# Routed experts with the first product two tiles ahead, two chunks to a PSUM bank and three banks for the second product

## The chip, the core and the metric

The kernel runs on one core of a Trainium2 chip. The metric is the time on the device in microseconds (us), the median of the runs. TensorE (PE in the rows) multiplies, VectorE (DVE), ScalarE (ACT) and GpSimd (POOL) work on what it leaves, SyncE (SP) starts transfers. The engines run programs of their own and meet at semaphores.

## What is computed

A layer of gated cross attention and a mixture of experts, on 32 sequences of 128 tokens with 128 channels (4096 tokens):

```python
x = x + tanh(g_xattn) * attention(layernorm(x), ctx, ctx, mask)      # 16 heads of 8
x = x + tanh(g_ffn) * ffn(layernorm(x))

def ffn(x):                                     # 2 shared experts, 8 routed ones, hidden size 512
    shared = mean over s of gelu(x @ sW1[s] + sb1[s]) @ sW2[s] + sb2[s]
    gates = x @ rW + rb
    w = softmax of the two largest gates, zero elsewhere
    moe = sum over e of w[e] * (gelu(x @ W1[e] + b1[e]) @ W2[e] + b2[e])
    return shared + moe
```

Only the two experts that a token chose are computed for it.

## The kernel before

The program has four stages: attention (with the gates), the shared experts, the routed experts, and the sum that ends the kernel. Every product of the experts is made of three matmuls in 16 bits: each operand is split into a high and a low half, and high times high, low times high and high times low are added in PSUM.

For the routed experts the rows of the tokens are scattered to slots in HBM, sorted by expert, each expert's slots filled up to a multiple of 256. That makes NTILE = 39 tiles of 256 slots, each of one expert, whose number stands in a register. For tile i:

- SP loads its rows into XR[i % 8] as soon as the results of tile i - 8 have been scattered (line 489).
- TensorE turns them into columns, four transposes into one PSUM buffer, rowT (`row_transposes`, line 1101). ScalarE copies them to XE[i % 3] (`routed_copy`, line 797). There is one rowT: the transposes of a tile wait until the tile before has been copied (semaphore XE).
- `routed_up`, line 1111, the first product: four chunks c of 128 hidden channels, three matmuls of 256 columns each. Chunk c goes to a PSUM bank of its own, pU[c] (pS0, pS1, pE0, pE1), in its first half. It waits for the activation of the same chunk of the tile before (semaphore gelu) and announces each chunk (semaphore up).
- `routed_gelu`, line 803: ScalarE takes each chunk to G32[i % 2], four activations of 128x256.
- `routed_split`, lines 1519 and 1521: VectorE makes high and low halves of two chunks at a time, in HR[i % 3] (semaphores hi, lo).
- `routed_down`, line 1123, the second product: 24 matmuls of 128 columns in pA[i % 2], the first 12 after the first half of the split, the rest after the second (semaphore dn).
- `routed_result`, line 1529: VectorE takes them to Y[i % 8] (semaphore y), and GpSimd scatters them with two indirect transfers (line 622) to HBM.

The order on each engine is written out by hand. I call it a step i. In step i TensorE does the first product of tile i + 1, the transposes of tile i + 3 and the second product of tile i; ScalarE the activations of tile i + 1 and the copy of tile i + 3; VectorE the split of tile i + 1 and the result of tile i.

Of the kernel before, what the change touches and what calls it, by code (L numbers as in the profile page):

```python
# [231 lines left out]
def layer(nc, io, k):  # L232
# [52 lines left out]
    G32 = [lt(f"G32{u}", [P, NC, TILE]) for u in range(2)]  # L285
    HR = [lt(f"HR{u}", [P, 2, NC, TILE], F16) for u in range(M)]
    Y = [lt(f"Y{u}", [P, 2, D]) for u in range(N)]
# [12 lines left out]
    pU = [wide(t) for t in (*pS, *pE)]  # L300
    pQK = lambda op: pM[:, 2 * op:2 * op + 2, :].rearrange("p a b -> p (a b)")
# [92 lines left out]
    with nc.Block() as block:  # L394
# [232 lines left out]
        def _(act):  # L627
# [166 lines left out]
            def routed_copy(i):  # L794
                act.wait_ge(r.T, i + 1)
                wait(act, r.up, NC * (i - M + 1))
                act.activation(XE[i % M][:], rowT, ACT.Copy).then_inc(r.XE, 1)

            def routed_gelu(i, e, c):
                act.wait_ge(r.up, NC * i + c + 1)  # L800
                if c % 2 == 0:
                    wait(act, r.lo, NC // 2 * (i - 2) + c // 2 + 1)
                act.activation(G32[i % 2][:, c, :], pU[c][:, 0:TILE], ACT.Gelu, bias=k.b1T[:, bass.ds(e * NC + c, 1)], scale=k.inv[:, 3:4]).then_inc(r.gelu, 1)  # L803

# [3 lines left out]
            for c in range(NC):  # L808
                routed_gelu(0, es[0], c)
            for i in range(NTILE):  # L810
# [16 lines left out]
        def _(pe):  # L827
# [276 lines left out]
            def routed_up(i, e):  # L1104
# [3 lines left out]
                for c in range(NC):  # L1108
                    wait(pe, r.gelu, NC * (i - 1) + c + 1)
                    for step, (w, part) in enumerate(((k.W1h, 0), (k.W1l, 0), (k.W1h, 1))):  # L1110
                        ins = pe.matmul(pU[c][:, 0:TILE], w[:, bass.ds(e * HID + c * P, P)], XE[i % M][:, part, :], start=(step == 0), stop=(step == 2))  # L1111
                    ins.then_inc(r.up, 1)

            def routed_down(i, e):
                wait(pe, r.y, i - 1)
                if i == 0:
                    pe.wait_ge(h.ot, NGR)
                for c in range(NC):
                    if c % 2 == 0:
                        pe.wait_ge(r.lo, NC // 2 * i + c // 2 + 1)  # L1120
                    for q in range(2):
                        for step, (w, part) in enumerate(((k.W2h, 0), (k.W2l, 0), (k.W2h, 1))):
                            ins = pe.matmul(pA[i % 2][:, q, :], HR[i % M][:, part, c, q * P:(q + 1) * P], w[:, bass.ds(e * HID + c * P, P)],  # L1123
# [9 lines left out]
            routed_up(0, es[0])  # L1133
            for i in range(NTILE):
# [7 lines left out]
        def _(v):  # L1142
# [371 lines left out]
            def routed_split(i):  # L1514
                for half in range(2):
                    ch = slice(2 * half, 2 * half + 2)
                    v.wait_ge(r.gelu, NC * i + 2 * half + 2)
# [107 lines left out]
```

## Time and profile before

| what | us |
|---|---|
| median of 3 runs | 527.5 (526.09 to 529.23) |
| profiled execution, its span | 524.9 |
| attention, ahead of the shared experts | to about 260 |
| shared experts | to about 362 |
| routed experts, the 39 tiles | 364.7 to about 504 |
| last scatters, loads and sums | to 524.9 |

A page of a profile gives the share of the span in which each engine is busy. Beside it stand views of the same execution by stretch, by wait, and in order of time. A wait is put down to whoever ended it; "issue" is an engine that waited for nothing the profile shows, and "remote" or "another core or an unknown queue" is a release for which the profile has no record at that time. The start of a matmul is recorded, its end is modelled. 2.6 us lie between the span and the median.

### The profile page before, as it was taken

What the parts mean: (1) busy time and instruction counts of PE and PEld (TensorE: products, weight loads), DVE (VectorE), ACT (ScalarE), POOL (GpSimd) and SP (SyncE); (2) the same over time, 40 slices, a digit from 0 to 9 for tenths busy, and PEclk for the clock granted to TensorE, in tenths of its full rate; (3) what the DMA queues carried; (4) which work ended last, traced back from release to release, by engine and by line L of the source; (5) the groups of instructions that cost most, each with busy time, mean ns of one, the idle gap of its engine ahead of it and who ended that gap; (6) DMA issues with size and microseconds to landing.
All of it is one profiled execution on the core that took longest, in us unless ns stands there. A gap on an engine that the chain in (4) does not pass through costs nothing.

```text
span 524.9 us, 13531 instructions
## 1 busy us (share of the span) xinstructions
PE 415.9 (79%) x4611; PEld 297.2 (57%) x4611; DVE 397.8 (76%) x983; ACT 340.8 (65%) x674; POOL 315.9 (60%) x382
## 2 busy tenths in 40 slices
PE   0377979879998989776784989898999989998930
PEld 0245767758776877554341433344878777776720
DVE  7696769868778778987774896494888768886795
ACT  0536857657787877665663876495677567765743
POOL 9151524494987889598876376650466656666550
PEclk9998989899999999988997989999999999999985
DMA  8767863442333534540011011113122222244119
GB/s 226 223 197 202 223 146 80 103 101 75 78 87 84 114 82 142 178 164 17 26 51 45 27 41 41 47 36 81 36 78 77 70 72 86 67 132 138 58 44 280
DMA packets 71753, 53.19 MB, mean 101 GB/s; under 512 B 7473, under 2 KB 63548, under 8 KB 71688
## 3 DMA queue, kind: packets, MB, share of 16 engines
q1 hardware_dynamic: 64608, 42.96, 30.2%
q0 software_dynamic: 4544, 8.44, 4.6%
q10 hardware_dynamic: 2536, 0.94, 0.7%
q8 instruction: 39, 0.64, 0.6%
q14 instruction: 26, 0.21, 0.2%
HBM read 29.38 MB, written 24.33 MB: 102 GB/s over the span
## 4 chain that ended last, share of the span: by engine, by line
PE 25%; DVE 8%; issue 5%; another core or an unknown queue 5%; ACT 4%; POOL 2%; DMA 1%; ACTq 0%; DVEq 0%; POOLq 0%
PE pAtt L1123 9%; PE pE L1111 4%; PE pS L1111 4%; DVE HH L1490 3%; PE pAtt L1061 2%; PE pMix L1101 2%; PE pS L999 2%; ACT H L767 1%; POOL yd L622 1%; PE pE L999 1%; DVE HH L1486 1%; ACT G L803 1%; DMA YY<-yd 1%; DVE t_X L1543 1%
## 5 line engine op out<-in xcount | busy, mean ns | idle before, releaser
L622 POOL DMA_INDIRECT yd<-Y,XR x78 | 85.0, 1089 | 72.5 <-DVE Y L1529 45.4
L1234 DVE TENSOR_REDUCE t_MX<-pS 128x4 f32<-128x512 f32 x128 | 86.4, 682 | 24.0 <-PE pS L861 22.4
L720 ACT ACTIVATE PT<-pE,t_mbias,t_scl 128x512 f32<-128x512 f32 x128 | 97.1, 788 | 6.6 <-PE pE L861 6.4
L597 POOL DMA_INDIRECT xs<-t_STG,t_pos x64 | 64.2, 1002 | 36.5 <-issue 15.4
L1123 PE MATMUL pAtt<-t_W2h,HR 128*128 x624 | 65.3, 219 | 6.8 <-issue 5.5
L803 ACT ACTIVATE G<-pS,t_b1T,t_inv 128x256 f32<-128x256 f32 x78 | 40.0, 569 | 43.6 <-remote 39.3
L1490 DVE SCALAR_TENSOR_TENSOR HH<-H,t_sc,HH 128x512 f16<-128x512 f32 x64 | 48.4, 761 | 21.6 <-ACT HH L772 14.7
L1521 DVE SCALAR_TENSOR_TENSOR HR<-G,t_sc,HR 128x512 f16<-128x512 f32 x78 | 58.6, 751 | 2.8
L1123 PE MATMUL pAtt<-t_W2l,HR 128*128 x312 | 56.4, 219 | 3.4 <-issue 3.4
L1123 PEld LDWEIGHTS pAtt<-t_W2h,HR 128*128 128x128 f16 x624 | 50.0, 97 | 12.6 <-issue 10.9
L861 PE MATMUL pE<-t_Q,t_K 128*128 128x128 f16 x512 | 51.6, 225 | 5.8 <-DMA t_Q<-MPT 4.8
L861 PE MATMUL pS<-t_K,t_Q 128*128 128x128 f16 x512 | 51.2, 225 | 4.1 <-DVE t_MX L1234 3.9
L1519 DVE TENSOR_SCALAR HR<-G,t_sc 128x512 f16<-128x512 f32 x78 | 37.5, 480 | 11.1 <-ACT G L803 11.1
L861 PEld LDWEIGHTS pE<-t_Q,t_K 128*128 128x128 f16 x512 | 37.1, 101 | 12.2 <-DMA t_Q<-MPT 5.3
L1061 PE MATMUL pAtt<-HH,t_W2h 128*128 128x512 f16 x128 | 38.2, 380 | 5.9 <-DVE HH L1490 3.6
L898 PE MATMUL pAtt<-PT,t_V 128*32 128x128 f32 x1024 | 42.8, 287 | 0.0
L522 POOL CAST QKS<-QK 128x512 f16<-128x512 f32 x16 | 9.8, 610 | 53.8 <-ACT QK L638 53.8
L803 ACT ACTIVATE G<-pE,t_b1T,t_inv 128x256 f32<-128x256 f32 x78 | 40.2, 578 | 0.0
L861 PEld LDWEIGHTS pS<-t_K,t_Q 128*128 128x128 f16 x512 | 34.6, 101 | 8.7 <-DVE t_MX L1234 7.8
L767 ACT ACTIVATE H<-pS,t_b1T,t_inv 128x512 f32<-128x512 f32 x32 | 23.6, 777 | 20.0 <-remote 13.6
L1529 DVE SCALAR_TENSOR_TENSOR Y<-pAtt,t_down,t_b 128x256 f32<-128x256 f32 x39 | 18.7, 480 | 20.5 <-remote 19.5
L1111 PE MATMUL pE<-XE,t_W1h 128*128 128x256 f16 x156 | 33.8, 274 | 0.0
(276 smaller groups left out, 1044.5 us busy)
## 6 DMA issues: line engine op xcount, KB each, us to landing
xs<-t_padrow SPq DMA_DIRECT2D x10, 516.0 KB, 5.3
XR<-xs SPq DMA_DIRECT2D x39, 129.0 KB
scr<-QKS SPq DMA_DIRECT2D x16, 256.0 KB, 2.2
t_Q<-scr SPq DMA_DIRECT2D x16, 256.0 KB
t_K<-scr SPq DMA_DIRECT2D x32, 128.0 KB
t_STG<-in_W SPq DMA_DIRECT2D x7, 512.0 KB, 6.4
YY<-yd SPq DMA_DIRECT2D x14, 256.0 KB, 5.8
t_X<-in_x SPq DMA_DIRECT2D x4, 512.0 KB, 6.5
```

Of the source, the lines that this page charges most:

```text
L597: g.indirect_dma_start(k.xs, bass.IndirectOffsetOnAxis(ap=pos[:, n:n + 1], axis=0), k.PAY[:, n, :], None).then_inc(h.di[q], 16)
L622: g.indirect_dma_start(k.yd, bass.IndirectOffsetOnAxis(ap=XR[u][:, q, D:ROW], axis=0), Y[u][:, q, :], None, bounds_check=2 * T - 1, oob_is ...
L720: act.activation(PT[:, m % NPT], pE[g % 2][:], ACT.Exp, bias=k.mbias[:, bt:bt + 1], scale=k.scl[:, bt:bt + 1]).then_inc(s.exp, 1)
L803: act.activation(G32[i % 2][:, c, :], pU[c][:, 0:TILE], ACT.Gelu, bias=k.b1T[:, bass.ds(e * NC + c, 1)], scale=k.inv[:, 3:4]).then_inc(r.g ...
L861: ins = pe.matmul(out[:, j, :], ko if transposed else qo, qo if transposed else ko, start=True, stop=True)
L898: ins = pe.matmul(pA[bb][32 * j:32 * j + 32, part // 2, :], k.V[pair % NB][:, 4 * bb + j, part, :], PT[:, m % NPT, j, :], start=(part == 0 ...
L1061: ins = pe.matmul(wide(pA[u]), w[:, w0:w0 + P], HH[e][:, part, c, :], start=(e == 0 and c == 0 and step == 0), stop=(e == 1 and c == NC - ...
L1111: ins = pe.matmul(pU[c][:, 0:TILE], w[:, bass.ds(e * HID + c * P, P)], XE[i % M][:, part, :], start=(step == 0), stop=(step == 2))
L1123: ins = pe.matmul(pA[i % 2][:, q, :], HR[i % M][:, part, c, q * P:(q + 1) * P], w[:, bass.ds(e * HID + c * P, P)], start=(c == 0 and q == ...
L1234: v.tensor_reduce(out=MX[:, n % G // 4, m % 2, m // 2::2], in_=pS[n % 2][:], axis=AX_X, op=ALU.max).then_inc(s.max, 1)
L1490: v.scalar_tensor_tensor(out=HH[e][:, 1, c, :], in0=H32[:, c, :], scalar=k.sc[:, 2:3], in1=HH[e][:, 0, c, :], op0=ALU.mult, op1=ALU.subtra ...
L1521: v.scalar_tensor_tensor(out=HR[i % M][:, 1, ch, :], in0=G32[i % 2][:, ch, :], scalar=k.sc[:, 2:3], in1=HR[i % M][:, 0, ch, :], op0=ALU.mu ...
```

## The change

Three things are done together, all in the routed stage:

- TensorE and ScalarE work two tiles ahead of the second product. In step i TensorE does the first product of tile i + 2, the transposes of tile i + 4 and the second product of tile i; ScalarE the activations of tile i + 2 and the copy of tile i + 4; VectorE the split of tile i + 2 and the result of tile i.
- The first product puts two chunks into one bank: a tile fills two of the four banks, and even and odd tiles use different pairs. It announces two chunks at a time and waits for two at a time, of tile i - 2. ScalarE waits and announces likewise, still with four activations.
- The second product goes round three banks (pA0, pA1, pO), G32 gets a third buffer and HR a fourth. They lie in tiles of the shared experts (pO, H32, HH0), so each waits once, at its first use, until that stage is done with it.

XR and Y stay at eight buffers, XE at three, rowT at one. The count of matmuls, activations and vector instructions is the same.

```diff
+    G32.append(H32[:, :, 0:TILE])
+    HR.append(HH[0][:, :, :, 0:TILE])
+    NG, NH = len(G32), len(HR)
...
+    up_out = lambda i, c: pU[i % 2 * 2 + c // 2][:, c % 2 * TILE:(c % 2 + 1) * TILE]
+    down_out = lambda i: (*pA, pO)[i % 3][:, 0:2, :]
...
             def routed_gelu(i, e, c):
-                act.wait_ge(r.up, NC * i + c + 1)
+                if i == 2 and c == 0:
+                    act.wait_ge(h.lo, NC * SUNITS)
                 if c % 2 == 0:
-                    wait(act, r.lo, NC // 2 * (i - 2) + c // 2 + 1)
+                    act.wait_ge(r.up, NC // 2 * i + c // 2 + 1)
+                    wait(act, r.lo, NC // 2 * (i - NG) + c // 2 + 1)
...
             for i in range(NTILE):
-                if i + 1 < NTILE:
+                if i + 2 < NTILE:
                     for c in range(NC):
-                        routed_gelu(i + 1, es[i + 1], c)
-                if i + 3 < NTILE:
-                    routed_copy(i + 3)
+                        routed_gelu(i + 2, es[i + 2], c)
+                if i + 4 < NTILE:
+                    routed_copy(i + 4)
...
                 for c in range(NC):
-                    wait(pe, r.gelu, NC * (i - 1) + c + 1)
+                    if c % 2 == 0:
+                        wait(pe, r.gelu, NC // 2 * (i - 2) + c // 2 + 1)
...
-                        ins = pe.matmul(pU[c][:, 0:TILE], w[:, bass.ds(e * HID + c * P, P)], XE[i % M][:, part, :], start=(step == 0), stop=(step == 2))
-                    ins.then_inc(r.up, 1)
+                        ins = pe.matmul(up_out(i, c), w[:, bass.ds(e * HID + c * P, P)], XE[i % M][:, part, :], start=(step == 0), stop=(step == 2))
+                    if c % 2:
+                        ins.then_inc(r.up, 1)
...
             def routed_down(i, e):
-                wait(pe, r.y, i - 1)
+                wait(pe, r.y, i - 2)
+                if i == 2:
+                    pe.wait_ge(h.x, NGR)
...
             for i in range(NTILE):
-                if i + 1 < NTILE:
-                    routed_up(i + 1, es[i + 1])
-                if i + 3 < NTILE:
-                    row_transposes(i + 3)
+                if i + 2 < NTILE:
+                    routed_up(i + 2, es[i + 2])
+                if i + 4 < NTILE:
+                    row_transposes(i + 4)
                 routed_down(i, es[i])
...
+            routed_split(1)
             for i in range(NTILE):
-                if i + 1 < NTILE:
-                    routed_split(i + 1)
+                if i + 2 < NTILE:
+                    routed_split(i + 2)
                 routed_result(i, es[i])
```

TensorE at the head of step 33, before (the last matmul of the second product of tile 32, then the first product of tile 34; XE and pS, pE are numbered by buffer):

```order
L1123 MATMUL pAtt0<-t_W2h,HR2 128x128
L1111 ISA [waits x_gelu,x_XE]
L1111 MATMUL pS0<-XE1,t_W1h 128x256
L1111 REGISTER_ALU
L1111 MATMUL pS0<-XE1,t_W1l 128x256
L1111 MATMUL pS0<-XE1,t_W1h 128x256
L1111 ISA [waits x_gelu]
L1111 MATMUL pS1<-XE1,t_W1h 128x256
```

The same place after, where the first product is that of tile 35:

```order
L1139 MATMUL pOut<-t_W2h,HR0 128x128
L1124 ISA [waits x_gelu,x_XE]
L1124 MATMUL pE0<-XE2,t_W1h 128x256
L1124 REGISTER_ALU
L1124 MATMUL pE0<-XE2,t_W1l 128x256
L1124 MATMUL pE0<-XE2,t_W1h 128x256
L1124 ISA
L1124 MATMUL pE0<-XE2,t_W1h 128x256
```

Chunks 0 and 1 share pE0, and the wait for an activation stands before every second chunk.

TensorE in the middle of step 33, before: the end of the first product of tile 34, the transposes of tile 36 (rows of XR4), the start of the second product of tile 33:

```order
L1111 MATMUL pE1<-XE1,t_W1h 128x256
L1101 MATMUL pMix<-t_ident16,XR4 128x128 [waits x_XE,x_ld4]
L1101 MATMUL pMix<-t_ident16,XR4 128x128 x3
L1123 REGISTER_ALU [waits x_lo,x_y]
L1123 MATMUL pAtt1<-t_W2h,HR0 128x128
```

The same place after: first product of tile 35, transposes of tile 37 (XR5), second product of tile 33:

```order
L1124 MATMUL pE1<-XE2,t_W1h 128x256
L1113 MATMUL pMix<-t_ident16,XR5 128x128 [waits x_XE,x_ld5]
L1113 MATMUL pMix<-t_ident16,XR5 128x128 x3
L1139 REGISTER_ALU [waits x_lo,x_y]
L1139 MATMUL pAtt0<-t_W2h,HR1 128x128
```

The transposes have moved with the first product, by one tile, and still wait for the copy of the tile before theirs.

ScalarE around the activations of tile 16, before; the last row is the copy of tile 18:

```order
L797 ACTIVATE XE2<-pMix 128x512 [waits x_up,x_T]
L803 ISA [waits x_lo,x_up]
L803 ACTIVATE G320<-pS0,t_b1T,t_inv 128x256
L803 ISA [waits x_up]
L803 ACTIVATE G320<-pS1,t_b1T,t_inv 128x256
L803 ISA [waits x_lo,x_up]
L803 ACTIVATE G320<-pE0,t_b1T,t_inv 128x256
L803 ISA [waits x_up]
L803 ACTIVATE G320<-pE1,t_b1T,t_inv 128x256
L797 ACTIVATE XE0<-pMix 128x512 [waits x_up,x_T]
```

And after:

```order
L802 ACTIVATE XE2<-pMix 128x512 [waits x_up,x_T]
L810 ISA [waits x_lo,x_up]
L810 ACTIVATE G321<-pS0,t_b1T,t_inv 128x256
L810 ISA
L810 ACTIVATE G321<-pS0,t_b1T,t_inv 128x256
L810 ISA [waits x_lo,x_up]
L810 ACTIVATE G321<-pS1,t_b1T,t_inv 128x256
L810 ISA
L810 ACTIVATE G321<-pS1,t_b1T,t_inv 128x256
L802 ACTIVATE XE0<-pMix 128x512 [waits x_up,x_T]
```

In both the copy of tile 18 stands behind the activations of tile 16: both moved by one tile against the second product, neither against the other.

## Rows read from the trace of the kernel before

**Rows 1.** The page: span, and TensorE's busy time, share and instructions

```profile
span 524.9 us, 13531 instructions
...
PE 415.9 (79%) x4611; PEld 297.2 (57%) x4611; DVE 397.8 (76%) x983; ACT 340.8 (65%) x674; POOL 315.9 (60%) x382
```

**Rows 2.** Stretch of three tiles: length, engines' busy time, granted clock, DMA, GB/s

```profile
398.00:408.67 10.67, 9.85 (x124) 8.21 (x122) 8.25 (x16) 7.14 (x15) 6.55 (x7) 1.00 0.25 76
```

**Rows 3.** Chain of waits, 421 to 440 us: start, length, what (instructions)

```profile
425.94 0.66 PE pS L1111 x6
...
427.48 1.34 PE pAtt L1123 x24
428.82 0.66 PE pS L1111 x6
...
430.35 0.40 PE pAtt L1123 x7
430.75 0.41 issue
...
431.56 0.32 issue
...
432.76 0.14 issue
432.90 0.85 PE pS L1111 x6
...
434.66 0.38 PE pMix L1101 x4
435.03 1.58 PE pAtt L1123 x24
436.62 0.65 PE pS L1111 x6
```

**Rows 4.** Who waited for whom, 366 to 502: us, times, longest

```profile
ACT G L803 <- remote: 39.3, 12, 3.6
DVE Y L1529 <- remote: 19.5, 12, 1.7
```

**Rows 5.** ScalarE in order of time: start, length, instruction, [idle before]

```profile
428.22 0.61 ACT L797 ACTIVATE XE<-pMix 128x512 f16<-128x512 f16 x1
432.09 1.02 ACT L803 ACTIVATE G<-pS,t_b1T,t_inv 128x256 f32<-128x256 f32 x2 [3.27 <-remote]
...
433.90 0.61 ACT L797 ACTIVATE XE<-pMix 128x512 f16<-128x512 f16 x1
```

**Rows 6.** VectorE in order of time, the same three tiles

```profile
429.69 0.75 DVE L1521 SCALAR_TENSOR_TENSOR HR<-G,t_sc,HR 128x512 f16<-128x512 f32 x1
432.05 0.48 DVE L1529 SCALAR_TENSOR_TENSOR Y<-pAtt,t_down,t_b 128x256 f32<-128x256 f32 x1 [1.60 <-remote]
```

**Rows 7.** GpSimd in order of time, first scatters of two tiles in a row

```profile
426.10 1.26 POOL L622 DMA_INDIRECT yd<-Y,XR  x1 [1.00 <-issue]
...
428.95 1.17 POOL L622 DMA_INDIRECT yd<-Y,XR  x1 [0.30 <-issue]
```

**Rows 8.** Shared experts in order of time: TensorE's last matmul, ScalarE's next activation

```profile
337.25 0.38 PE L1061 MATMUL pAtt<-HH,t_W2l 128*128 128x512 f16 x1
...
338.37 0.78 ACT L767 ACTIVATE H<-pS,t_b1T,t_inv 128x512 f32<-128x512 f32 x1 [6.38 <-remote]
```

**Rows 9.** Load of tile 8's rows as issued, and its transposes, in order of time

```profile
376.53 0.36 SPq L489 DMA_DIRECT2D XR<-xs  x1
...
384.30 0.39 PE L1101 MATMUL pMix<-t_ident,XR 128*128 128x128 f16 x4
```

**Rows 10.** The page's DMA issues: count, KB each, median us from issue to landing

```profile
YY<-yd SPq DMA_DIRECT2D x14, 256.0 KB, 5.8
...
scr<-QKS SPq DMA_DIRECT2D x16, 128.0 KB, 2.3
```

More of the change, by code:

```diff
@@ L809, in _ @@
                 routed_gelu(0, es[0], c)
+            routed_copy(3)
+            for c in range(NC):
+                routed_gelu(1, es[1], c)
             for i in range(NTILE):
-                if i + 1 < NTILE:
+                if i + 2 < NTILE:
                     for c in range(NC):
-                        routed_gelu(i + 1, es[i + 1], c)
-                if i + 3 < NTILE:
-                    routed_copy(i + 3)
+                        routed_gelu(i + 2, es[i + 2], c)
+                if i + 4 < NTILE:
+                    routed_copy(i + 4)
             for n in range(NQ):
@@ L1122, in routed_down @@
                         for step, (w, part) in enumerate(((k.W2h, 0), (k.W2l, 0), (k.W2h, 1))):
-                            ins = pe.matmul(pA[i % 2][:, q, :], HR[i % M][:, part, c, q * P:(q + 1) * P], w[:, bass.ds(e * HID + c * P, P)],
+                            ins = pe.matmul(down_out(i)[:, q, :], HR[i % NH][:, part, c, q * P:(q + 1) * P], w[:, bass.ds(e * HID + c * P, P)],
                                             start=(c == 0 and q == 0 and step == 0), stop=(c == NC - 1 and step == 2), skip_group_check=True)
@@ L1516, in routed_split @@
                     ch = slice(2 * half, 2 * half + 2)
-                    v.wait_ge(r.gelu, NC * i + 2 * half + 2)
-                    wait(v, r.dn, i - M + 1)
-                    v.tensor_scalar(HR[i % M][:, 0, ch, :], G32[i % 2][:, ch, :], k.sc[:, 2:3], None, ALU.mult).then_inc(r.hi, 1)
+                    v.wait_ge(r.gelu, NC // 2 * i + half + 1)
+                    wait(v, r.dn, i - NH + 1)
+                    if i == NH - 1:
+                        v.wait_ge(h.dn, SUNITS)
+                    v.tensor_scalar(HR[i % NH][:, 0, ch, :], G32[i % NG][:, ch, :], k.sc[:, 2:3], None, ALU.mult).then_inc(r.hi, 1)
                     v.wait_ge(r.hi, 2 * i + half + 1)
-                    v.scalar_tensor_tensor(out=HR[i % M][:, 1, ch, :], in0=G32[i % 2][:, ch, :], scalar=k.sc[:, 2:3], in1=HR[i % M][:, 0, ch, :],
+                    v.scalar_tensor_tensor(out=HR[i % NH][:, 1, ch, :], in0=G32[i % NG][:, ch, :], scalar=k.sc[:, 2:3], in1=HR[i % NH][:, 0, ch, :],
                                            op0=ALU.mult, op1=ALU.subtract).then_inc(r.lo, 1)
@@ L1528, in routed_result @@
                 row = k.b2[:, bass.ds(e * D, D)].rearrange("p (o d) -> p o d", o=1)
-                v.scalar_tensor_tensor(out=Y[u][:], in0=pA[i % 2][:, 0:2, :], scalar=k.down[:, 0:1], in1=row.to_broadcast([P, 2, D]),
+                v.scalar_tensor_tensor(out=Y[u][:], in0=down_out(i), scalar=k.down[:, 0:1], in1=row.to_broadcast([P, 2, D]),
                                        op0=ALU.mult, op1=ALU.add).then_inc(r.y, 1)
```

8 lines of the change are left out of this document (6 added, 2 removed).

## The prediction

> **What bounds the kernel now.** I began with the page: TensorE is busy 79% of the span, more than any other engine [rows 1], and the change touches nothing ahead of the routed stage. So I read that stage alone, first cut into stretches. Stretches of 10.67 us look alike from 377 to 494 us, and each holds three tiles, at a granted clock of 1.00, that is 2.4 GHz [rows 2]. In one of them the engines work 9.85 us (TensorE), 8.25 (VectorE), 7.14 (ScalarE) and 6.55 (GpSimd): none is full, TensorE nearly.
>
> The chain of waits shows what one such stretch is made of [rows 3]. First products begin at 425.94, 428.82, 432.90 and 436.62, so the three intervals are 2.88, 4.08 and 3.72 us. The first is TensorE back to back: 1.31 for the first product, 0.22 for the transposes, 1.34 for the second product. If every interval were 2.88, the stretch would take 8.64; it takes 10.68. **2.04 us are lost every three tiles**, and only that can be won.
>
> Where do they go? The views of waits name it: ScalarE waits 12 times, 39.3 us in all, on "remote", and VectorE waits 12 times, 19.5 us, on the same [rows 4]. In the stretch shown the first product of a tile starts at 428.82 and its first chunk is through by about 429.2. ScalarE has been free since its copy of 428.22, yet starts on that chunk at 432.09, after 3.27 us of idleness [rows 5]. VectorE finishes its split at 430.44 and starts the result of the tile before at 432.05, though that tile's second product was recorded as over at 428.82 [rows 6]. Both wait for semaphores that TensorE sets, and both get them at the same moment. So once in three tiles what TensorE has finished is announced some 3 us late. I call this the **late release**. TensorE itself goes on for a while in its records, then stops twice inside the second product, 0.41 and 0.32 us, for nothing the profile shows, and then goes at ScalarE's pace: 0.14 us of waiting, 1.76 instead of 1.31 for the next first product, 0.38 instead of 0.22 for the transposes, 1.59 instead of 1.34 for the second product behind them [rows 3].
>
> The Trainium skill says in Perfetto Trace Analysis, Tensor Engine Instruction, that the recorded end of a matmul is an estimate and that the semaphore goes out only when PSUM has acknowledged the writes. The rows agree that recorded end and release are two things; that they can lie 3 us apart no page told me.
>
> **The change, part by part.** The number of matmuls, activations, splits and scatters is the same, so the busy times stay. What it takes away or adds:
>
> *Waits of the first product.* Now each chunk waits for the same chunk of the tile before; after the change, for a pair of chunks two tiles back. In the stretch this removes the 0.14 and the 0.45 (1.76 less 1.31) that follow the late release [rows 3].
>
> *The transposes.* This is the wait that takes its place. Transposes of tile i + 4 need the copy of tile i + 3, which ScalarE makes behind the activations of tile i + 1. Before, those of tile i + 3 needed the copy of tile i + 2, behind the activations of tile i. In both, TensorE may be ahead of ScalarE by one tile less a first product, and no more. With the release at 432.09 as now, the four activations and the copy end at 433.90 + 0.61 = 434.51 [rows 5]. The transposes then start at about 434.60, where today they start at 434.66. Two tiles of lead, and the transposes move by 0.06 us.
>
> *The second product.* It is no longer paced by a split that has only just come: 1.34 instead of 1.59. The transposes take 0.22 instead of 0.38. So the next first product but one starts at 434.60 + 0.22 + 1.34 = 436.16 instead of 436.62 [rows 3]: **0.46 us gained per late release**. The two stops inside the second product, 0.73 us, don't count, either way: they lie before 434.60, where ScalarE is later than TensorE.
>
> *VectorE and GpSimd.* VectorE needs 8.25 us for three tiles [rows 2], 2.75 a tile. GpSimd begins two tiles in a row at 426.10 and 428.95 [rows 7], 2.85 a tile. Both are below 2.88, so neither sets a pace slower than TensorE's. But they are so near that a faster stage than 2.88 isn't to be had, and after a late release VectorE catches up only slowly. That costs nothing while its split is a tile ahead of the second product, which the fourth HR gives.
>
> *Two chunks at once.* ScalarE may start 0.33 us later on a tile, half of a pair's 0.66 [rows 3]. It has 7.14 of work in 10.67 us and a lead of a tile, so this is hidden, except behind a late release, where both chunks are long through. I take zero; the bound is 12 times 0.33, 4 us.
>
> *The ends.* At the start one more first product, 1.31 us, stands before the first second product. At the end two second products run with nothing between. The amount of work is the same, so I take zero, bounds -1 and +1.3. The one-time waits for pO, H32 and HH0 are on work of the shared stage that is over before tile 2 gets there: zero.
>
> *The loads of the rows.* The transposes come one tile earlier against the second product, while the load still waits for the scatter of eight tiles before. For tile 8 the load is issued at 376.53 and used at 384.30 [rows 9], 7.8 us later. One tile of 3.56 less leaves 4.2. No row gives the landing of these 129 KB; 128 KB of another kind take 2.3 and 256 KB 5.8 [rows 10]. By size it is nearest to the first: it fits. The second would not.
>
> **The sum.** 12 late releases times 0.46 are 5.5 us. On the profiled execution 524.9 - 5.5 = 519.4; the median of the runs lies 2.6 above its span, so 527.5 - 5.5 = **522.0**.
>
> **The rivals.**
>
> *The late release is absorbed.* If it has to do with how ScalarE and TensorE meet chunk by chunk, or ends earlier when TensorE waits less, all intervals become 2.88: 12 times 2.04 are 24.5 us, **503.0**. For it: two of three tiles already run near that pace, and half of the announcements and waits go. Against it: rowT keeps the two engines coupled, and the late release isn't seen to follow from a wait.
>
> *It isn't late at all: TensorE's work truly takes 10.67 us for three tiles*, and its records run ahead of it. Then nothing that reorders its work helps, **527.5**. For it: semaphores are what the other engines see. Against it: the release is prompt for two tiles in three, and between the releases there is not time enough for more. The Trainium skill gives a price by which this would be so, in TensorE: Matmul & The Clock Gate, Back-to-back issue gap: about 81 ns for a matmul of 128 columns with its weights. The 24 of the second product would take 1.9 us by it; the row says 1.34 for the 24 [rows 3].
>
> *The late release grows with TensorE's lead.* In the shared stage ScalarE waited 6.38 us for one and got it at 338.37, 0.74 us after TensorE's last matmul ended (337.25 + 0.38) and it had nothing more to do [rows 8]. If the release comes only when TensorE stops, a longer lead makes it later. TensorE would now run on to the transposes, at 428.82 + 2.88 + 1.31 = 433.01; the release would come at 433.75, activations and copy would end 2.42 later at 436.2, and 3.2 us would be lost instead of 2.04: 12 times 1.16 more, 13.9, **541.4**. It decides as soon as the release follows TensorE's stop. Against it: in the stretch shown TensorE stops in the middle of a product, where nothing asks it to.
>
> *The loads come too late.* If the rows land later than 4.2 us after issue, TensorE waits for them at the transposes. Four steps lie between a result and the transposes that reuse its place, so a lateness of x costs x/4 a tile. Landing at 5.0 us gives 0.2 a tile, over 37 tiles 7.4 less the 5.5 gained: **529.4**; at 5.8 it is 0.4 a tile, 14.8 less 5.5, 536.8.
>
> **How the numbers follow.** The forecast of 522.0 gets 0.40, with a range of its own from 518 to 526 (the zero terms above are its bounds). Absorbed: 0.20. TensorE truly full: 0.17. Grows with the lead: 0.13. Loads late: 0.10. 0.5% is 2.6 us, about what a measurement of this kernel can tell from no change. Faster by more: 0.37 of the forecast and the 0.20, 0.57. Within: 0.03 of the forecast and the 0.17, 0.20. Slower: 0.23. The range from 502 to 534 takes in the absorbed case and the late loads but for their worst, and leaves out 0.13 and a little.
>
> **What would show it.** In the profile after, the stretches should still repeat every three tiles, in about 10.2 us. ScalarE should still wait 12 times about 3 us for a release without a record. TensorE should no longer wait before the first product but before the transposes, for the copy, once in three tiles. The second product should take 1.34 everywhere. If ScalarE's unexplained waits are gone, the first rival holds; if stretches take 10.67 with TensorE waiting for nothing, the second; if the waits are longer than 4 us, the third; if the transposes wait for a transfer, the fourth. The forecast is wrong above all if the release isn't tied to a time but to what TensorE does next.

## The result

The changed kernel takes 531.25 us (median of 19 runs, 526.21 to 536.13) against 528.33 us before (19 runs, 525.99 to 535.18). The ratio is 1.0046, with a 95% interval of 1.0024 to 1.0068: by it 2.4 us slower, where 5.5 us faster had been forecast.

The page of the changed kernel, its first line and its line of busy times, answers to [rows 1]:

```profile
span 534.4 us, 13529 instructions
...
PE 414.2 (78%) x4611; PEld 301.9 (56%) x4611; DVE 398.4 (75%) x983; ACT 341.5 (64%) x674; POOL 315.5 (59%) x382
```

This execution was a disturbed one (granted clock 0.937, against 0.955 in the profile of before), so its span isn't compared, and only what repeats inside the stage is read from it. Who waited for whom, 370 to 511 us (total, times, longest), answers to [rows 4]:

```profile
ACT H L810 <- remote: 37.1, 11, 4.5
...
DVE Y L1549 <- remote: 17.1, 11, 1.8
```

The late releases are still there, eleven instead of twelve and about as long. The chain of waits of one stretch of three tiles (start, length, what) answers to [rows 3]:

```profile
443.48 0.51 issue
443.99 0.38 PE pMix L1113 x4
444.38 1.39 PE pAtt L1139 x24
445.77 1.31 PE pS L1124 x12
447.08 0.22 PE pMix L1113 x4
447.30 1.34 PE pOut L1139 x24
448.64 1.31 PE pE L1124 x12
...
454.26 0.54 issue
454.79 0.38 PE pMix L1113 x4
```

First products take 1.31 us each and no longer wait; TensorE now waits in front of the transposes, 0.51 and 0.54 us. So far it is what the forecast described, but for the transposes and the second product behind the wait, which take 0.38 and 1.39 us and not 0.22 and 1.34. But from transposes to the same transposes it is 454.79 - 443.99 = 10.80 us, not 10.2. The line that explains it wasn't TensorE's. GpSimd in order of time, the same stretch, answers to [rows 7]:

```profile
446.11 1.26 POOL L627 DMA_INDIRECT yd<-Y,XR  x1 [1.00 <-issue]
447.68 0.98 POOL L627 DMA_INDIRECT yd<-Y,XR  x1 [0.30 <-issue]
448.96 1.17 POOL L627 DMA_INDIRECT yd<-Y,XR  x1 [0.30 <-issue]
450.44 0.98 POOL L627 DMA_INDIRECT yd<-Y,XR  x1 [0.30 <-issue]
453.42 1.21 POOL L627 DMA_INDIRECT yd<-Y,XR  x1 [2.00 <-DVE Y L1549]
```

And ScalarE's first activations behind two late releases in a row:

```profile
441.43 1.93 ACT L810 ACTIVATE H<-pS,t_b1T,t_inv 128x256 f32<-128x256 f32 x4 [3.23 <-remote]
...
452.23 1.93 ACT L810 ACTIVATE H<-pE,t_b1T,t_inv 128x256 f32<-128x256 f32 x4 [3.26 <-remote]
```

Four scatters run back to back, from 446.11 to 451.42; the release comes at 452.23, 0.81 us after the last of them has ended. Then GpSimd waits for a result, which VectorE couldn't make before the release. Of this **train of four** the forecast had seen only that 2.85 us a tile is less than 2.88.

### The profile page after: what moved, and what is told of

It is laid out like the page before. It is cut to its first block, busy times and chain, and to the rows that moved or that the text cites. A ratio compares the mean times of both kernels' runs of the same rounds, so it can differ in the third digit from the quotient of the medians.

```text
span 534.4 us, 13529 instructions
## 1 busy us (share of the span) xinstructions
PE 414.2 (78%) x4611; PEld 301.9 (56%) x4611; DVE 398.4 (75%) x983; ACT 341.5 (64%) x674; POOL 315.5 (59%) x382
## 4 chain that ended last, share of the span: by engine, by line
PE 32%; DVE 22%; ACT 11%; issue 10%; another core or an unknown queue 8%; DMA 7%; POOL 4%; SPq 1%; ACTq 1%; DVEq 0%; POOLq 0%
PE pAtt L1139 4%; DVE HH L1508 4%; PE pS L1124 3%; DVE t_MX L1252 3%; DMA kwm<-t_tops 3%; PE pE L1124 3%; PE pAtt L910 3%; ACT G L810 2%; PE pE L873 2%; ACT H L772 2%; PE pS L873 2%; PE pMix L854 2%; PE pOut L1139 2%; PE pAtt L1073 1%
## 5 line engine op out<-in xcount | busy, mean ns | idle before, releaser
L910 PE MATMUL pAtt<-PT,t_V 128*32 128x128 f32 x1024 | 43.9, 292 | 0.0
L1139 PE MATMUL pAtt<-t_W2h,HR 128*128 x320 | 33.6, 220 | 4.1 <-issue 4.0
L1124 PE MATMUL pS<-XE,t_W1h 128*128 128x256 f16 x160 | 31.9, 285 | 0.6 <-issue 0.6
L1011 PE MATMUL pS<-t_STG,t_W1h 128*128 128x512 f16 x64 | 23.8, 411 | 10.1 <-ACT H L772 10.1
L1139 PE MATMUL pAtt<-t_W2l,HR 128*128 x160 | 29.2, 220 | 2.9 <-issue 2.9
L1541 DVE SCALAR_TENSOR_TENSOR HR<-G,t_sc,HR 128x512 f16<-128x512 f32 x40 | 30.0, 751 | 1.4
L1139 PEld LDWEIGHTS pAtt<-t_W2h,HR 128*128 128x128 f16 x320 | 25.7, 98 | 7.5 <-issue 7.4
L910 PEld LDWEIGHTS pAtt<-PT,t_V 128*32 128x32 f32 x1024 | 25.4, 114 | 7.2 <-issue 1.0
L810 ACT ACTIVATE G<-pE,t_b1T,t_inv 128x256 f32<-128x256 f32 x52 | 25.5, 580 | 4.7 <-PE pE L1124 2.6
L1124 PE MATMUL pE<-XE,t_W1h 128*128 128x256 f16 x152 | 28.0, 273 | 0.0
```

Source lines behind the costliest of these rows:

```text
L810: ins = act.activation(G32[i % NG][:, c, :], up_out(i, c), ACT.Gelu, bias=k.b1T[:, bass.ds(e * NC + c, 1)], scale=k.inv[:, 3:4])
L910: ins = pe.matmul(pA[bb][32 * j:32 * j + 32, part // 2, :], k.V[pair % NB][:, 4 * bb + j, part, :], PT[:, m % NPT, j, :], start=(part == 0 ...
L1124: ins = pe.matmul(up_out(i, c), w[:, bass.ds(e * HID + c * P, P)], XE[i % M][:, part, :], start=(step == 0), stop=(step == 2))
L1139: ins = pe.matmul(down_out(i)[:, q, :], HR[i % NH][:, part, c, q * P:(q + 1) * P], w[:, bass.ds(e * HID + c * P, P)], start=(c == 0 and q ...
```

## What the experiments had to tell apart

The experiments ran on seven chips, and these are of two kinds. On four (besides that of the first result) the kernel before takes 525.6 to 533.0 us, on three 484.1 to 486.4, and one of the three gave 484.14 and 485.13 at two times. Both kinds run the same program. I call them **chips of 526** and **chips of 486**. Every time below stands beside that of the kernel before on the same chip.

Theories: (a) TensorE's work truly takes 10.67 us for three tiles; (b) its sequencer is the limit, which computes an address for every matmul of the routed stage; (c) GpSimd's scatters hold up its semaphores; (d) it takes the other engines' work on PSUM; (e) the single buffer rowT holds back the lead, as the forecast said; and for the loss, (f) late loads and (g) the ends of the stage.

### TensorE alone

```diff
-                wait(pe, r.XE, i)
+                wait(pe, r.XE, min(i, 3))
-                    wait(pe, r.gelu, NC * (i - 1) + c + 1)
+                    if i == 1:
+                        pe.wait_ge(r.gelu, c + 1)
-                wait(pe, r.y, i - 1)
...
-    HR[i % M][:, part, c, q * P:(q + 1) * P]
+    HR[0][:, part, c, q * P:(q + 1) * P]
```

and the loops of the other engines over the tiles end after the first ones, so what such a kernel returns isn't the layer's result. Three such kernels ran on chips of 486:

> The kernel before, in whose routed stage only TensorE goes through all 39 tiles: transposes, first and second products as before, in the same order, but on the rows, the XE and the HR of the first tiles, so that after tile 0 it waits for nobody. Copies, activations and splits after the first tiles, results, scatters and all but the first eight loads are left out; the last stage adds up other data. Theory 'TensorE is full' (its work truly takes 10.67 us for three tiles): the 38 tiles behind the first take 3.56 us each also when nobody holds it up, first product to first product, some 135 us. Theory 'the late release comes from outside TensorE' (from another engine's or a queue's work, or from the way it meets ScalarE): 2.88 us each, some 109 us, in the records as in what the last semaphore tells, whose waiters are the loads of the last stage. Where the records run ahead of the truth, the loads begin later than the last recorded matmul by more than the 1 us that a semaphore and a DMA start may take.

> As the run with TensorE alone, but the weights of both products stand at a fixed place (expert 0) rather than at one computed from a register; the same parts are left out. If TensorE's sequencer is the limit (it computes an address for every matmul of the routed stage, 36 a tile), the tiles become shorter than in that run, by up to the 3.56 to 2.88 us. If it is the array or the loading of weights, both runs have the same length per tile.

> TensorE alone in the routed stage once more (the same parts left out as in the first run of it), wanted on a chip on which the kernel before takes some 526 us. Theory 'it is TensorE itself that stops on such a chip, whatever the others do': the 38 tiles take 3.56 us each, 135 us, seen at the latest in the time between the first routed product and the loads of the last stage, which wait for its last semaphore. Theory 'it takes the other engines': 2.87 us each, 109 us.

And one on a chip of 526:

> TensorE alone in the routed stage (the same parts left out as in the first run of it), for the case that this call gets a chip of 526 us. Theory 'TensorE itself stops on such a chip': 3.56 us a tile, 135 us for 38 tiles. Theory 'it takes the other engines': 2.87 us, 109 us. On a chip of 486 us 2.87 us a tile is known already.

Measured: 488.15, 486.28 and 486.06 us on the chips of 486 (before: 486.36, 486.36, 484.98), and 504.53 on the chip of 526 (before: 526.5). The third is a median of 8 runs, the others are one run each. TensorE's weight loads for the first products, with first and last start, on the chip of 526:

```profile
L1096 PEld LDWEIGHTS pS<-XE,t_W1h x156: 95/98/98, 366.0 to 474.8; 128*128 x156
```

The same with fixed weights on a chip of 486:

```profile
L1096 PEld LDWEIGHTS pS<-XE,t_W1h x156: 96/98/98, 347.6 to 456.4; 128*128 128x128 f16 x156
```

108.8 us for both. Busy times of 20 us on the chip of 526 (length; PE, PEld, DVE, ACT, POOL; granted clock; DMA share; GB/s):

```profile
380.00:400.00 20.00, 20.00 (x281) 19.06 (x280) 0.00 (x0) 0.00 (x0) 0.00 (x0) 1.00 0.01 2
```

TensorE never stops, and the loads that wait for its last semaphore were issued at 478.50 us, 0.03 us after its last recorded matmul had ended. So (a) falls, on the very kind of chip that has the late releases, and with it the second rival of the prediction. (b) falls with it, since the registers were in use. The 22 us that this run saves against before there fit what the late releases of the routed stage cost, 12 times 2.04 = 24.5, less what the last stage adds when nothing overlaps it; no run parts the two. The other 18 us between the chips (first routed product at 366.0 and 347.6) lie ahead of the routed stage.

### Fixed weights, everything else at work

```diff
-    w[:, bass.ds(e * HID + c * P, P)]
+    w[:, c * P:c * P + P]
```

> The kernel before with the weights of both routed products at a fixed place (expert 0 for all tiles), so its results are those of other weights; all the rest is as before. Theory 'sequencer': the stretches of three tiles fall from 10.67 us towards 8.64, up to 24 us off the whole, about 503. Theory 'something else makes the release late': 10.67 stays, 527 to 528.

The chip was one of 486: 484.61 us, ratio 0.9974 (0.9932 to 1.0016). It can't speak on the late release. But its profile shows the kernel before where that is absent. Who waited for whom, 340 to 470 us:

```profile
POOL yd L622 <- issue: 23.2, 76, 0.3
...
ACT G L803 <- PE pS L1111: 17.4, 37, 1.0
```

There is no "remote". GpSimd scatters without a pause (76 of 78 start 0.3 us behind the one before) and first products come every 2.87 us. Here the scatters stand in far longer trains, and on this chip they harm nothing.

This profile also shows where most of the 18 us ahead of the stage go. GpSimd's first scatter of the program, which brings rows to their slots, starts at 241.3 us here and at 242.5 us in the kernel before on a chip of 526 (the profile of the next section). From there to the first routed product it is 105.5 and 121.2 us. In the longer one, in the shared experts, ScalarE waits (total, times, longest):

```profile
ACT H L767 <- remote: 18.6, 5, 7.9
```

and in the shorter one never. So late releases stand in the shared experts too, where GpSimd scatters as well (the granted clock there is 0.93, against 1.00 here). But they don't all wait for a train to end: one of the five came at 276.43 us, in the middle of 19 scatters in a row from 259.27 to 284.12.

### Before and after once more, both kinds of chip

> The kernel before, for a profile of it on the chip of this call. In the first call's chip TensorE's neighbours never waited in the routed stage and the whole took 486.36 us instead of 528.33. Theory 'the late release belongs to the chip, not to the kernel': on a chip of 486 us every tile takes 2.87 us and no wait of 3 us for a release without a record is there; on a chip of 528 us they come once in three tiles, as in the first profile.

> The changed kernel, timed against the kernel before on the chip of this call. On a chip without late releases TensorE is full in the routed stage (2.87 us a tile, no stop), so a longer lead has nothing to win: theory 'it only helps what waits' gives 1.000, bounds -1 and +1.3 us for the two ends of the stage. On a chip with late releases the 1.0046 of the first result should come again, +2.4 us.

> The changed kernel again, wanted on a chip of 486 us. The two-row variant took 1.1% more than before there, and its chain of waits ran from a scatter's landing through the load of XR (4.3 us from issue to landing) to TensorE's transposes. Theory 'the change makes the loads of the rows late, and the slow chips hide it under the late releases': the changed kernel too is slower than before on such a chip, by 2 to 6 us (487 to 491). Theory 'it only helps what waits': the same as before. On a chip of 526 us it repeats the 1.005 of the two results there.

> The changed kernel, wanted on a chip of 486 us. TensorE is full there with the kernel before, 2.87 us a tile. Theory 'loads of the rows come late': transposes wait for XR as in the two-row run, 487 to 491, that is 0.3 to 1.1% slower. Theory 'nothing to win, nothing lost': 1.000. On a chip of 526 us it repeats 1.0045 to 1.006.

On chips of 526: 528.71 us against 525.6, ratio 1.0063 (1.0027 to 1.0100), and 529.18 against 526.5, ratio 1.0045 (1.0013 to 1.0076). On a chip of 486: **492.66 against 485.13, ratio 1.0147** (1.0068 to 1.0226). The theory "it only helps what waits", with 1.000 there, falls.

Where it goes shows when the stage is cut at three instructions, each with its first and last start: VectorE's result, TensorE's transposes, GpSimd's scatter. Before, chip of 526:

```profile
L1529 DVEq FUSED_REGOPS  x39: 57/57/65, 369.6 to 503.5; - x39
...
L1101 PE MATMUL pMix<-t_ident,XR x156: 216/219/219, 361.2 to 491.1; 128*128 128x128 f16 x156
...
L622 POOLq MOVE  x78: 29/29/29, 370.8 to 504.6; - x78
```

Changed, same chip:

```profile
L1549 DVEq FUSED_REGOPS  x39: 57/57/65, 368.7 to 499.7; - x39
...
L1113 PE MATMUL pMix<-t_ident,XR x156: 216/219/315, 356.7 to 486.9; 128*128 128x128 f16 x156
...
L627 POOLq MOVE  x78: 29/29/29, 369.9 to 502.0; - x78
```

Changed, chip of 486:

```profile
L1549 DVEq FUSED_REGOPS  x39: 57/57/65, 357.1 to 466.5; - x39
...
L1113 PE MATMUL pMix<-t_ident,XR x156: 216/219/311, 344.9 to 456.8; 128*128 128x128 f16 x156
...
L627 POOLq MOVE  x78: 29/29/29, 358.3 to 468.8; - x78
```

| us | chip | first transposes to first result | first to last result | last result to last scatter | sum |
|---|---|---|---|---|---|
| before | 526 | 8.4 | 133.9 | 1.1 | 143.4 |
| changed | 526 | 12.0 | 131.0 | 2.3 | 145.3 |
| changed, another chip | 526 | 11.3 | 133.3 | 2.2 | 146.8 |
| before, fixed weights | 486 | 8.5 | 107.6 | 1.1 | 117.2 |
| changed | 486 | 12.2 | 109.4 | 2.3 | 123.9 |

The first result comes 2.9 to 3.7 us later and the last scatter 1.1 to 1.2 us. On chips of 526 the middle takes back 0.6 to 2.9; on the chip of 486 it costs 1.8 more (against the kernel with fixed weights, the one profile there is of before on such a chip), although TensorE starts it with a longer lead.

Part of the 3.6 at the start is the clock. TensorE's very first product of the stage, changed kernel, in the profiles with 12.0 and with 11.3 us (length; PE, PEld, DVE, ACT, POOL; granted clock; DMA share; GB/s):

```profile
359.40:361.80 2.40, 2.40 (x15) 1.75 (x13) 0.00 (x0) 1.31 (x3) 0.00 (x0) 0.52 0.03 7
...
363.20:365.60 2.40, 2.40 (x26) 2.06 (x25) 0.07 (x1) 1.79 (x4) 0.00 (x0) 1.00 0.03 7
```

The first ran at 1.2 GHz, the second at 2.4, and so did that of both profiles of before in the table. At the same clock the start costs 2.9: 2.4 for one more split on VectorE, and 0.5 from the transposes to the first split, most likely because ScalarE now gets chunks in pairs.

In the middle there are eleven late releases in every profile of the changed kernel on chips of 526, and twelve before. The first two lie 22 to 23 us apart and the first of them comes inside a train of six scatters or more than a us behind one of four; behind it, as before, each comes 0.6 to 1.05 us after a train of four has ended. From one to the next it is 10.67 to 10.77 us before but for one of 11.0 in each profile, and 10.65 to 10.85 after, but for the profile on the other chip, where it is 10.91 to 10.99 in seven of nine. Nowhere is it 10.2.

Who waited for whom on the chip of 486, 344 to 480 us:

```profile
PEld pMix L1113 <- DMA XR<-xs: 5.9, 6, 2.0
PE pMix L1113 <- DMA XR<-xs: 4.1, 3, 1.8
```

and the chain of waits into one such wait:

```profile
371.61 3.59 DMA yd<-Y,XR
375.21 3.19 DMA XR<-xs
378.44 0.40 PE pMix L1113 x4
```

The scatter of tile i - 8 takes 3.6 us from its start to its landing, 2.6 of them behind its recorded end at 372.59, then the load of XR takes 3.2, then the transposes follow. The Trainium skill says, in Perfetto Trace Analysis, DMA Instruction — SWDGE (GPSIMD), that a scatter's recorded end is the end of making its descriptors and not of moving the data; the trace agrees, with 2.6 to 3.7 us from the recorded end to the landing in the four such places of this chain. That is theory (f), in the trace; no run takes the wait away on a chip of 486.

### Two buffers for the transposed rows

```diff
-    rowT = pM[:, 0:2, :]...
+    rowT = [t[:, 0:2, :]... for t in (pM, pO)]
-    down_out = lambda i: (*pA, pO)[i % 3][:, 0:2, :]
+    down_out = lambda i: pA[i % 2][:, 0:2, :]
-                wait(pe, r.XE, i)
+                wait(pe, r.XE, i - 1)
```

> The changed kernel with the one thing that the forecast said was holding its lead back: two buffers for the transposed rows (the second in pOut) instead of one, so that transposes wait for the copy two tiles back. The second product goes back to two banks for it. By the forecast's mechanism TensorE could then run a tile further behind a late release, and 2.04 us per late release would shrink: up to 24 us off, about 503. Theory 'TensorE stops by itself, the waits of the others are only its shadow': 10.7 us for three tiles stay, 526 to 529 on a slow chip; on a chip of 486 us all stay at 486.

A chip of 486: 491.72 us against 484.98, ratio 1.011 (1.0046 to 1.0174), slower, with transposes waiting for XR as in the changed kernel. On such a chip there is no late release to shrink, so (e) wasn't tried where it matters and stays untested.

### Results stored by plain DMAs instead of scatters

```diff
+            def store_result(i):
+                sp.wait_ge(r.y, i + 1)
+                sp.dma_start(yrows[i % (2 * T // TILE)], Y[i % N][:]).then_inc(r.st[i % N], 16)
...
-                for q in range(2):
-                    g.indirect_dma_start(k.yd, ...).then_inc(r.st[u], 16)
```

> The kernel before, in whose routed stage GpSimd scatters nothing: each tile's results are stored by one plain DMA from SyncE's queue, and the last stage adds up rows of x. The bytes stay. On a chip of 526 us: theory 'the scatters hold up TensorE's semaphores' gives no late release, tiles of 2.87 us, about 503; theory 'TensorE stops by itself' gives 10.67 us for three tiles as before, about 526. On a chip of 486 us neither has anything to show, and the run tells only whether the plain stores cost something, 486.

> The kernel before, in whose routed stage GpSimd scatters nothing: each tile's results are stored by one plain DMA from SyncE's queue, and the last stage adds up rows of x; wanted on a chip of 526 us, where TensorE alone (a run that also had no scatters) took 2.87 us a tile. Theory 'the scatters that GpSimd starts hold up TensorE's semaphores': no late release in the routed stage, 2.87 to 2.9 us a tile, and as the late releases ahead of the stage stay, about 505. Theory 'it takes ScalarE's or VectorE's work on PSUM': 10.7 us for three tiles as before, about 526. On a chip of 486 us it repeats 487.5.

The last stage adds up rows of x, so this isn't the layer's result either. It ran three times, on two chips of 486: 487.47 against 484.98, 487.91 against 484.14, and a single run of 487.43 against 485.13. So it told nothing on the release. A probe with TensorE alone and tiny listeners on ScalarE and VectorE ran twice (485.63 and 486.33 us) on one of these chips and has no wait on "remote" at all, scatters or not:

> TensorE alone as in the runs of that name, with listeners: ScalarE answers the first and the last chunk of every tile with a tiny activation, VectorE every second product with a tiny copy, so that the time of each semaphore's arrival stands in the trace. Nothing holds TensorE up. Tiles 1 to 9 have only the listeners; in tiles 10 to 18 GpSimd scatters two blocks of rows of x a tile; in 19 to 27 ScalarE (4 activations) and VectorE (4 splits) work on SBUF; from 28 on SyncE loads 128 KB a tile. The stage's other work is left out. On a chip of 526 us: theory 'scatters' has listeners of tiles 10 to 18 wait some 3 us once in three tiles, and all others answer within 0.2 us; theory 'work on SBUF' has it in 19 to 27; theory 'DMA' from 28 on; if all are prompt, it takes PSUM reads or waits of TensorE. On a chip of 486 us all are prompt.

Then one kernel that has both ways in one execution, tiles 12 to 25 scattered by GpSimd, the others stored by SyncE:

```diff
+    by_sp = lambda i: i < 12 or i >= 26
...
+                if by_sp(i):
+                    continue
                 g.wait_ge(r.y, i + 1)
```

> The kernel before, in whose routed stage the tiles 12 to 25 are scattered by GpSimd as always and the results of tiles 0 to 11 and 26 to 38 are stored by plain DMAs (two of 64 KB a tile) from SyncE's queue; the last stage adds up rows of x. Wanted on a chip of 526 us: both ways stand in one execution. Theory 'the scatters hold up TensorE's semaphores': late releases of about 3 us once in three tiles from tile 12 or 13 to 25 or 26 alone, and 2.87 us a tile in the first and last part but for late loads. Theory 'ScalarE's or VectorE's work on PSUM': late releases all through the stage. On a chip of 486 us none in any part.

It ran on a chip of 526: **513.04 us against 533.03**, one run each. Who waited for ScalarE's gelus and VectorE's results, first 372 to 405 us, where the tiles are stored by SyncE:

```profile
ACT G L824 <- PE pS L1132: 5.2, 12, 0.5
```

then 405 to 460 us, where GpSimd scatters:

```profile
ACT G L824 <- remote: 16.4, 5, 3.4
...
DVE Y L1550 <- remote: 8.7, 5, 1.8
```

ScalarE behind the first and the last of the five late releases:

```profile
411.57 1.02 ACT L824 ACTIVATE G<-pS,t_b1T,t_inv 128x256 f32<-128x256 f32 x2 [2.82 <-remote]
...
454.81 1.02 ACT L824 ACTIVATE G<-pS,t_b1T,t_inv 128x256 f32<-128x256 f32 x2 [3.39 <-remote]
```

and TensorE's busy time in the two parts, 28.74 and 43.24 us long:

```profile
372.00:400.74 28.74, 28.74 (x403) 27.38 (x401) 27.86 (x51) 24.19 (x51) 0.00 (x0) 1.00 0.32 86
411.57:454.81 43.24, 39.08 (x485) 32.38 (x483) 32.98 (x61) 28.57 (x61) 26.22 (x24) 1.00 0.27 80
```

The first part is ten tiles at 2.87 us with no stop; the second has 12 at 3.60, its releases 10.81 us apart. Behind it, 460 to 500 us, there is no "remote" again. **In the routed stage of this execution no late release stands without scatters, and they begin and end with them.** That is (c), and (d) falls: ScalarE and VectorE read PSUM in both parts. Whether it is GpSimd's part of a scatter or the transfer, this run can't tell.

### Nine buffers for the rows, and the result ahead of the split

```diff
+    XR.append(OT[:, 0:2 * ROW].bitcast(I32).rearrange("p (q w) -> p q w", w=ROW))
```

> The changed kernel with nine buffers for the rows' loads instead of eight (the ninth lies in OTs, unused by then), so that a load waits for the scatter of nine tiles before: the tile of slack that the earlier transposes took is given back. Theory 'loads are late': on a chip of 486 us TensorE's waits for XR are gone and the time is that of the kernel before, within 0.5%, and below the changed kernel's. Theory 'something else of the change costs': the same as the changed kernel. On a chip of 526 us, where a load has 4 us more, no difference from the changed kernel is expected by either.

On a chip of 526: 531.03 us, ratio 1.0091 (1.0051 to 1.0131), beside 1.0045 (1.0013 to 1.0076) of the changed kernel on the same chip. The intervals overlap; it brought nothing there, as expected. Then the same, with

```diff
-                if i + 2 < NTILE:
-                    routed_split(i + 2)
                 routed_result(i, es[i])
+                if i + 2 < NTILE:
+                    routed_split(i + 2)
```

> The changed kernel with nine buffers for the rows' loads, and with VectorE making the result of tile i ahead of the split of tile i + 2 instead of behind it. Two claims on where the change loses, seen apart in the trace. Start: the first result now waits for one more split, 2.4 us; it should begin 12.2 - 2.4 = 9.8 us behind the first transposes instead of 12.2 (the kernel before: 8.5), on any chip. Loads: on a chip of 486 us TensorE's waits for XR (six, the longest 2.0 us, in the changed kernel) should be gone. Theory 'start, end and loads are all that the change costs': on a chip of 486 us 1.000 to 1.005 of the kernel before instead of 1.015; on a chip of 526 us, where the loads have slack and the period of 10.67 us belongs to GpSimd, 0.998 to 1.002 instead of 1.0045. Theory 'something else costs': 1.0045 and more on a slow chip, 1.01 and more on a fast one.

Again a chip of 526: 531.93 against 529.51, ratio 1.0058 (1.0023 to 1.0093). Both ends are as expected: the first result comes 8.7 us behind the first transposes instead of 11.3 at the same clock, 2.6 where 2.4 was expected, and the last scatter is 1.2 behind the last result. (g) is right on its place. Yet the kernel gained nothing, because the middle grew to 138.8 us. GpSimd in order of time:

```profile
404.46 1.26 POOL L633 DMA_INDIRECT yd<-Y,XR  x1 [2.03 <-DVE Y L1555]
406.03 0.98 POOL L633 DMA_INDIRECT yd<-Y,XR  x1 [0.30 <-issue]
407.32 1.17 POOL L633 DMA_INDIRECT yd<-Y,XR  x1 [0.31 <-issue]
408.79 0.98 POOL L633 DMA_INDIRECT yd<-Y,XR  x1 [0.30 <-issue]
411.86 1.26 POOL L633 DMA_INDIRECT yd<-Y,XR  x1 [2.09 <-DVE Y L1555]
```

and ScalarE behind two late releases:

```profile
403.27 1.93 ACT L816 ACTIVATE G<-pS,t_b1T,t_inv 128x256 f32<-128x256 f32 x4 [2.62 <-remote]
410.66 1.94 ACT L816 ACTIVATE H<-pS,t_b1T,t_inv 128x256 f32<-128x256 f32 x4 [2.67 <-remote]
```

Each train of four is now followed by the next: two tiles in 7.40 us, 3.7 a tile instead of 3.56. The late release comes once in two tiles, still 0.89 us after a train has ended. It is tied neither to three tiles nor to three XE buffers, but to the trains. And the period is what the train and the wait behind it give: 5.31 us of scatters and 2.1 to the next, with no pair in between.

## Why the prediction was wrong

**What failed: "with the release at 432.09 as now".** The sum of the forecast, 0.46 us gained per late release, let everything behind the release come sooner and kept the release itself where it stood against TensorE's work. The runs put a closed loop in its place, and TensorE's lead isn't in it. A train of four takes 5.31 us. The release comes 0.6 to 1.05 us after its end. Then two things follow. VectorE makes the result it had waited for, and GpSimd, idle for 1.9 to 2.0, scatters its two blocks (2.5). And ScalarE makes activations, VectorE four halves of splits and only then the next result, and with that, 1.0 us after the pair, the next train begins, 4.7 us behind the release. 5.31 + 1.9 to 2.0 + 2.5 + 1.0 is 10.7 to 10.8, the period before (10.67) and after (10.80) in the first two profiles. That the four add up to it is no proof, since they fill it; that each starts what follows is read from the waits. The test is the kernel with the result ahead of the splits: it takes the pair and the second pause out of the loop, and two tiles then take 7.4 us. In the profile of the changed kernel on the other chip of 526 the pair comes sooner and the next train 5.0 us behind the release, and the period is mostly 10.91 to 10.99.

The term "12 times 0.46" measured: no shorter period in any profile, against 5.5 us won. What TensorE won it spent in front of the transposes. The 0.46 was too large by itself, too: the next first product but one started 4.53 us behind the release before (436.62 - 432.09) and starts 4.34 behind it after (445.77 - 441.43), 0.19 less. The transposes behind the wait still take 0.38 and the second product 1.39, where 0.22 and 1.34 had been put.

**"Both are below 2.88, so neither sets a pace slower than TensorE's"**, on VectorE and GpSimd, is the sentence that hid it. As a rate it is true, and on chips of 486 it is what one sees. But 2.85 of 2.87 us means back to back, and on a chip of 526 it is the train, not the rate, that costs. The rows of GpSimd were read for their starts alone. The last scatter of the train in the kernel before:

```profile
430.43 0.98 POOL L622 DMA_INDIRECT yd<-Y,XR  x1 [0.31 <-issue]
```

It ends at 431.41, 0.68 us ahead of the release of [rows 5], and the other eleven releases follow a train of four by 0.68 to 1.01 us.

**The ends: "I take zero, bounds -1 and +1.3"** failed too, and this is what made the kernel slower. Measured +3.6 and +2.9 at the start (chips of 526), +1.1 to +1.2 at the end. The start was costed for TensorE, whose extra first product is hidden behind VectorE's splits. Not seen was that VectorE's own order now has three splits ahead of the first result instead of two, 2.4 us; with the order turned round they were gone. Another 0.5 is most likely the term *Two chunks at once*, which was put at nothing as well, and 0.7 of the 3.6 is the lower clock. At the end two results come with nothing between them, and GpSimd, at 2.6 us a tile, has one more tile to finish.

**The waits named were right**: first products wait for nobody, transposes wait instead. "Two tiles of lead, and the transposes move by 0.06 us" was a good reading of rowT: they started 2.57 us behind the release before (434.66 - 432.09) and start 2.56 behind it after (443.99 - 441.43). Whether a second rowT would help on a chip of 526 no run shows.

**The rivals.** *Absorbed* (503.0) would have been the end of the late release; nothing in the change could do that, though plain stores did, for the tiles that had them. *Truly 10.67 us* (527.5) is refuted by TensorE alone. *Grows with the lead* is refuted: 3.26 us is still the wait. It had asked the right question, what the release follows, and looked for the answer in TensorE. Its own example, the release at 338.37 [rows 8], comes 0.27 us after the end of a train of twelve scatters that began at 322.70. *Loads late* gave the nearest time, 529.4, and that was luck: on chips of 526 the changed kernel's transposes waited for XR once in two of the three profiles, 0.3 and 0.9 us. Its mechanism stands on the chip of 486, with six waits, the longest 2.0 us, where it can cost up to the 1.8 us of the middle; no run takes it away there. The slack of 4.2 us was counted at 3.56 us a tile. At 2.87 the four steps are 2.8 us shorter, so an estimate from these numbers leaves 1.4 for a landing that took 3.2 in the chain above.

**What would have been right:** 12 times 0 for the late releases, +2.4 for the split ahead of the first result and +1.2 for the last tile, 3.6 us in all. The changed kernel was 2.4 to 3.3 us slower than before on its chips of 526. So near a hit leaves things out on both sides: 0.5 to 1.2 more at the start, and 0.6 to 2.9 that the middle gives back, with one late release less. Only two profiles measure that, against a single one of before, on the chip of the first.

**Open:** what differs between the chips; why a train of two scatters does no harm and one of four does, and what ends a late release inside a train, as in the shared experts and at the start of the changed kernel; which part of a scatter holds up the semaphores; whether scatters alone are enough, without ScalarE's and VectorE's work (the probe never ran on a chip of 526); whether a second rowT helps there; and whether nine buffers help on a chip of 486.

## What to carry to other kernels

When two engines wait for a third without a record, look at what all the others do at the moment when the wait ends, and compare it over several repeats: here a train of scatters ended 0.7 to 1.0 us ahead of each of twelve. A period that survives a change of lead belongs to a loop that the change isn't in, so find that loop before costing what the lead gives. And when a software pipeline is made one tile deeper, write out the first and the last tile of every engine, not of TensorE alone: each engine's own order may put one more tile of its work in front of the first result.

## What the runs showed of the hardware

The same program took 485 us on some chips and 527 on others, at the same granted clock of 1.00 in the routed stage and the same 2.87 us a tile when TensorE ran alone. What differs is when TensorE's semaphores reach ScalarE and VectorE while GpSimd scatters back to back: promptly on the one kind, some 3 us late once in a train of four on the other. Without the scatters the second kind, too, ran ten tiles at 2.87 us. On it the stage goes at the pace of the trains and of the releases behind them, although GpSimd is busy for only 6.55 us of 10.67 [rows 2].
